# Ranking edges by source bucket in half chunks: the match tile in PSUM, a predicated copy for product and addition

## The reference, cut to what matters

```python
src, dst = (edge_index[0], edge_index[1])
msg_input = jnp.concatenate([x[src], x[dst], edge_attr], axis=-1)
h = jax.nn.relu(msg_input @ W1.T + b1)
messages = h @ W2.T + b2
agg = jax.ops.segment_sum(messages, dst, num_segments=x.shape[0])
upd = jax.nn.relu(agg @ Wu.T + bu)
y = x + upd
```

## Time and profile before

| | us |
|---|---|
| median of 3 runs (lowest, highest) | 6159.68 (6158.24, 6160.03) |
| span of the profiled execution | 6159.3 |
| starts of the first and the last gather of the edge MLP | 1456.1, 2644.6 |
| starts of the first and the last match of the ranking | 1466.1, 2500.5 |

### The profile page before, as it was taken

How to read it: one execution, slowest core, us unless ns; L and a number is a source line. 1 busy time by engine, 2 the same in 40 slices (tenths; PEclk the granted TensorE clock), 3 DMA queues, 4 the chain that set the end, 5 groups by cost and what they waited for, 6 DMA issues and landing times. The chain is left out here.

```text
span 6159.3 us, 93437 instructions
## 1 busy us (share of the span) xinstructions
PE 3901.9 (63%) x20652; PEld 3181.0 (52%) x20652; DVE 3661.3 (59%) x11663; ACT 2833.9 (46%) x6936; POOL 4388.1 (71%) x4477
## 2 busy tenths in 40 slices
PE   5567766765666666768878877334444346766665
PEld 4566666654555555545655555233333346665443
DVE  6788888886888888767777675111101124445665
ACT  3788888881111111255555554111111148784443
POOL 3676777654777777757777776677777777777775
PEclk8787887787888888878898887555555569898877
DMA  4444444454645555542222224322222235553223
GB/s 125 124 132 126 129 128 127 127 103 125 171 133 136 139 136 134 145 66 73 74 74 74 74 74 66 96 77 76 76 75 75 74 108 167 163 165 88 58 58 46
DMA packets 485366, 649.31 MB, mean 105 GB/s; under 512 B 120187, under 2 KB 332938, under 8 KB 484822
## 3 DMA queue, kind: packets, MB, share of 16 engines
q0 software_dynamic: 155552, 345.75, 22.1%
q1 hardware_dynamic: 329271, 297.58, 17.7%
HBM read 495.44 MB, written 150.71 MB: 105 GB/s over the span
## 5 line engine op out<-in xcount | busy, mean ns | idle before, releaser
L692 POOL DMA_INDIRECT e_ring<-table,gather_i x880 | 921.5, 1047 | 287.3 <-issue 267.5
L692 POOL DMA_INDIRECT kv_ring<-keys_values,gather_i x880 | 864.1, 982 | 365.2 <-issue 248.0
L2099 POOL DMA_INDIRECT rows_by_src<-arena,key x880 | 870.9, 990 | 310.2 <-issue 260.3
L692 POOL DMA_INDIRECT e_ring<-filter_rows,gather_i x880 | 840.7, 955 | 304.5 <-issue 268.1
L692 POOL DMA_INDIRECT arena<-table,gather_i x880 | 858.7, 976 | 278.9 <-issue 265.9
L2083 PE MATMUL rs_ph<-nodes,arena 128*128 x1664 | 424.4, 436 | 668.1 <-ACT arena L2092 615.2
L2083 PEld LDWEIGHTS rs_ph<-nodes,arena 128*128 128x128 f32 x1664 | 365.7, 324 | 727.4 <-issue 727.2
L2075 DVE TENSOR_SCALAR arena<-arena,part 128x512 f32<-128x512 bf16 x220 | 113.2, 518 | 949.0 <-PE rs_ph L2083 898.8
L1562 PE MATMUL e_pa<-e_msg,e_hot 128*128 128x128 f32 x3520 | 559.9, 311 | 35.8 <-DVE e_msg L1764 28.2
L741 DVE TENSOR_TENSOR arena<-arena,e_pa 128x128 f32 x1760 | 495.0, 281 | 114.0 <-PE e_pa L1562 68.9
L2325 PE MATMUL gl_sum_f<-arena,gl_hot_f 128*128 128x128 f32 x1760 | 283.0, 311 | 425.0 <-DMA arena<-table,gather_i 191.0
(11 more groups left out here) (461 smaller groups left out, 9863.7 us busy)
## 6 DMA issues: line engine op xcount, KB each, us to landing
rows_by_src<-e_filler SPq DMA_DIRECT2D x256, 260.0 KB
arena<-rows_by_src SPq DMA_DIRECT2D x256, 260.0 KB
at_rows<-local_rows SPq DMA_DIRECT2D x220, 128.0 KB, 3.5
e_rows<-local_rows SPq DMA_DIRECT2D x220, 128.0 KB
arena<-local_rows SPq DMA_DIRECT2D x220, 128.0 KB, 3.3
e_attr<-edge_attr SPq DMA_DIRECT2D x880, 25.0 KB
kv_ring<-keys_values,gather_i POOLq DMA_INDIRECT x880
e_ring<-table,gather_i POOLq DMA_INDIRECT x880
```

The lines of the kernel that those rows point to most:

```text
L692: pool.indirect_dma_start(ring[:, r, u, :], None, table, bass.IndirectOffsetOnAxis(index, 0)).then_inc(arrived[r], 16)
L2099: pool.indirect_dma_start(self.table, bass.IndirectOffsetOnAxis(place, 0), self.out[:, r, u, :], None, bounds_check=SLOTS_R - 1, oob_is_er ...
```

## The change

The row of 832 columns is ranked in two halves of 416 (`HCHUNK`). For each half there are three instructions: the match, now written to a PSUM tile; the scan, which reads the match there and starts the second half from the last rank of the first; and a predicated copy, which writes the rank into `slot_of` where the match isn't zero (no two buckets mark the same edge, so a copy does what product and addition did). That is six instructions a bucket in the same four steps: in an even step the match comes ahead of all the step's other work and the scan at its end, in an odd step the copy comes at its end. Each still waits for the one before.

The match tile takes a bank of PSUM. `pn` goes from four banks to three: the result of `project` moves into columns 128 to 255 of the bank of `turn_nodes`. `turn_nodes` waits in addition until `keep_rows` of the bucket before has read it. SP's wait at batch 204 is for a count of 297 instead of 199.

```diff
--- before.py
+++ after.py
@@ -18,6 +18,7 @@
 F32 = mybir.dt.float32
 I32 = mybir.dt.int32
 BF16 = mybir.dt.bfloat16
+U32 = mybir.dt.uint32
 ALU = mybir.AluOpType
 ACT = mybir.ActivationFunctionType
 AX_X = mybir.AxisListType.X
@@ -82,6 +83,7 @@
 VALS0 = ACC_N
 LINKS0 = VALS0 + VALS * U * F
 RANKS0 = B1_0
+HCHUNK = CHUNK // 2
 SPOTS0 = RANKS0 + 5 * CHUNK
 NUMBERS0 = SPOTS0 + JC * P
 assert RANKS0 + 4 * TILES <= SPOTS0 and NUMBERS0 + 3 * TILES <= QUERY0
@@ -1321,7 +1323,7 @@
 
             filler, filled = sb("filler", [P, U, REV]), sem("filled")
             src_i = arena(c, RANKS0, [CHUNK], I32)
-            src_bucket, slot_of, match, rank = (arena(c, RANKS0 + n * CHUNK, [CHUNK]) for n in range(1, 5))
+            src_bucket, slot_of, rank = (arena(c, RANKS0 + n * CHUNK, [CHUNK]) for n in range(1, 4))
             sources, ranked, slotted, spotted = sem("sources"), sem("ranked"), sem("slotted"), sem("spotted")
             phase, whole = (arena(c, NUMBERS0 + n * TILES, [TILES]) for n in range(2))
             cut, sined = sem("cut"), sem("sined")
@@ -1329,7 +1331,8 @@
             sums, sums_t, plus, mid, y, t, z, x_new, x_t = (sb(n, [P, P]) for n in ("sums", "sums_t", "plus", "mid", "y", "t", "z", "x_new", "x_t"))
             keep = sb("keep", [P, 3, F])
             stat, mean, root = sb("stat", [P, 2, 6]), sb("mean", [P, 2, 2]), sb("root", [P, 2, 2])
-            pn = pb("pn", [P, 4, 512])
+            pn = pb("pn", [P, 3, 512])
+            match = pb("match", [P, 512])[:, 0:HCHUNK]
             joined, summed_t, copied_t, updated, added_x, moments, rooted = (sem(n) for n in ("joined", "summed_t", "copied_t", "updated", "added_x", "moments", "rooted"))
             shifted, moments2, renewed, turned_x, copied_x, projected, kept, held = (
                 sem(n) for n in ("shifted", "moments2", "renewed", "turned_x", "copied_x", "projected", "kept", "held"))
@@ -1398,7 +1401,7 @@
                     sp.dma_start(to, attr_dram[:, bass.ds(e0[u], P)]).then_inc(attributes[r], 16)
                 if layer == 1:
                     if k == R * NB + 8:
-                        sp.wait_ge(ranked, 3 + 4 * NB)
+                        sp.wait_ge(ranked, 3 + 6 * NB)
                         sp.dma_start(c.slots.rearrange("(p n) -> p n", p=P), slot_of).then_inc(slotted, 16)
                     if is_first(k):
                         sp.wait_ge(start, 3)
@@ -1480,7 +1483,7 @@
                 act.wait_ge(projected, n + 1)
                 at_least(act, row_sent[n % 3], 16 * (n // 3), None)
                 at_least(act, held, n - 2, None)
-                act.activation(keep[:, n % 3, :], pn[:, 3, 0:F], ACT.Copy).then_inc(kept, 1)
+                act.activation(keep[:, n % 3, :], pn[:, 2, P:P + F], ACT.Copy).then_inc(kept, 1)
 
             def soften_nodes(k, i, r):
                 n = BUCKET_AT.get(k)
@@ -1588,6 +1591,7 @@
                     return
                 pe.wait_ge(renewed, 2 * n + 1)
                 at_least(pe, copied_x, n, None)
+                at_least(pe, kept, n, None)
                 pe.transpose(pn[:, 2, 0:P], x_new[:, :], c.ident[:, :]).then_inc(turned_x, 1)
 
             def project(k, i, r):
@@ -1596,7 +1600,7 @@
                     return
                 pe.wait_ge(copied_x, n + 1)
                 at_least(pe, kept, n, None)
-                pe.matmul(pn[:, 3, 0:F], x_t[:, :], c.w["lin1"][:, :], start=True, stop=True).then_inc(projected, 1)
+                pe.matmul(pn[:, 2, P:P + F], x_t[:, :], c.w["lin1"][:, :], start=True, stop=True).then_inc(projected, 1)
 
             def mix(k, i, r):
                 n = BUCKET_AT.get(k)
@@ -1659,16 +1663,16 @@
                 dve.wait_ge(ranked, 2)
                 dve.tensor_scalar(slot_of, src_bucket, float(NB), float(4 * SLOTS), ALU.is_ge, ALU.mult).then_inc(ranked, 1)
 
-            def rank_bucket(b, part):
-                dve.wait_ge(ranked, 3 + b * 4 + part)
+            def rank_bucket(b, half, part):
+                dve.wait_ge(ranked, 3 + b * 6 + half * 3 + part)
+                of = slice(half * HCHUNK, half * HCHUNK + HCHUNK)
+                before_it = c.base[:, b:b + 1] if half == 0 else rank[:, HCHUNK - 1:HCHUNK]
                 if part == 0:
-                    ins = dve.tensor_scalar(match, src_bucket, c.j[:, b:b + 1], None, ALU.is_equal)
+                    ins = dve.tensor_scalar(match, src_bucket[:, of], c.j[:, b:b + 1], None, ALU.is_equal)
                 if part == 1:
-                    ins = dve.tensor_tensor_scan(rank, c.ones[:, 0:1].broadcast_to([P, CHUNK]), match, c.base[:, b:b + 1], ALU.mult, ALU.add)
+                    ins = dve.tensor_tensor_scan(rank[:, of], c.ones[:, 0:1].broadcast_to([P, HCHUNK]), match, before_it, ALU.mult, ALU.add)
                 if part == 2:
-                    ins = dve.tensor_tensor(rank, rank, match, ALU.mult)
-                if part == 3:
-                    ins = dve.tensor_tensor(slot_of, slot_of, rank, ALU.add)
+                    ins = dve.copy_predicated(slot_of[:, of], match.bitcast(U32), rank[:, of])
                 ins.then_inc(ranked, 1)
 
             def number(n):
@@ -1838,6 +1842,8 @@
                 new = not (isinstance(k, int) and k >= BATCHES)
                 there = lambda n: (not isinstance(k, int) or n <= k < BATCHES + n)
                 steps = []
+                if layer == 1 and k < R * NB and r % 2 == 0:
+                    rank_bucket(k // R, r // 2, 0)
                 if layer == 1 and new:
                     steps.append(lambda: one_hot_turned(k, i, r))
                 if layer == 2 and there(2):
@@ -1851,7 +1857,7 @@
                     return Adds(nc, dve, acc, buckets, pa[:, ra % 2, :, :], F, ka, summed, added, tick)
                 between(adds if there(add_lag) else None, steps)
                 if layer == 1 and k < R * NB:
-                    rank_bucket(k // R, r)
+                    rank_bucket(k // R, r // 2, 1 + r % 2)
                 if layer == 1 and CUT_AT <= k < CUT_AT + 4:
                     cut_off(k - CUT_AT)
                 if layer == 1 and CUT_AT + 8 <= k < CUT_AT + 10:
```

## The result

| | us |
|---|---|
| before, median of 4 runs beside it | 6159.85 |
| changed, median of 4 runs (lowest, highest) | 6080.08 (6069.62, 6084.35) |
| ratio, with its 95% interval | 0.9867 (0.9856 to 0.9879) |
| span of the profiled execution, the quickest of the four | 6067.6 |
| starts of the first and the last gather of the edge stage | 1451.6, 2564.3 |

A forecast was written before the change was run, and what follows sets the result against it. POOL's 880 gathers, one after another, were taken to bound the second layer's edge stage, stretched by DVE's ranking. 79 us less there and nothing elsewhere: 6159.7 - 79 = 6081 us, range 6067 to 6122 us.

The forecast's parts named there:

- The step that carried the forecast: Second layer's edge stage: 771 gathers in the ranking window fall from 1058 to 955 ns, 79.4 us off POOL.
- 2566 us: Sign that the forecast is right: the edge stage's last gather starts near this time, against 2644.6 us before.
- the same clock: Edge stage, 2520 to 2600 us: gathers after ranking take 955 ns with clock unchanged and no less DMA traffic.
- the rival in which PSUM frees nothing: Ranking pieces still stall gathers, but shorter ones less: 26 us gained, 6133 us; chance 0.06.
- the bounds: Ranking on DVE, per half: match 0.34 to 1.04 us, predicated copy 0.59 to 1.04 us.
- DVE's reserve: Ranking window: DVE's time to spare against POOL's pace shrinks from 0.7 to 0.34 us a batch.
- wanted it halved: Sign that the forecast is right: DVE's idle before its edge-stage sum (L1759), 132.1 us before, halves.
- the rival in which DVE becomes the pace: Copy and match cost their upper ends, DVE needs 5.15 us a batch: 58 us gained, 6102 us; chance 0.16.
- The copy doesn't hold the port: Rival: the predicated copy still holds the port, reading what it overwrites: 11 us of stall, 6092 us; chance 0.15.
- The slow copy: Rival: a predicated copy of 2.5 us makes DVE 39 us slower, 6198 us; chance of slower 0.05.
- The bank cost nothing: Node results sharing a PSUM bank: 2 us of room, at most 13 us of PE time, costed at nothing.

The follow-up runs named there:

- e7: Kernel before with only the predicated copy, over all 832 columns, replacing product and addition, match in SBUF: 6153.41 us, ratio 0.9994.
- e3: Changed kernel with product and addition, in halves, instead of the predicated copy, match still in PSUM: 6080.68 us, ratio 0.9874.
- e5: Changed kernel plus two unused additions of 416 columns a bucket, one input in PSUM, the other in SBUF: 6084.47 us, ratio 0.9869.
- e4: Changed kernel plus one unused addition of 832 columns a bucket, inputs and output in SBUF: 6103.28 us, ratio 0.9894.
- e1: Changed kernel with only the match tile moved back to SBUF, halves and predicated copy kept: 6109.36 us, ratio 0.9920.
- e9: Changed kernel with the last stage's row of column numbers copied once into PSUM for its one-hot comparison: 6057.42 us, ratio 0.9829.
- e10: The changed kernel itself, run again on the same chip as e9 as its measure: 6079.4 us, ratio 0.9865.
- e6: Changed kernel plus three unused additions in each half, one operand in PSUM: 6142.55 us, ratio 0.9962.
- e8: Match, product and addition in SBUF as in the kernel before, but in halves of 416 and the change's order: 6130.23 us, ratio 0.9935.
- e2: Kernel before with only the shared PSUM bank and its added wait, ranking untouched: 6162.76 us, ratio 1.0003.

## Why the prediction was right

**The bound and the stall.** The step that carried the forecast was 771 x (1058 - 955) ns = 79.4 us on POOL. The stage shortened by 76 us, the gathers by 1058 - 960 = 98 ns each, and the median of the runs by 79.8 us. The last start came at 2564.3 us, where 2566 us was named. That the forecast of the whole time is met to 1 us is luck: 76 us are the stage's, the other 4 us lie elsewhere, and the runs of the changed kernel spread over 15 us. e7 shows that DVE work taken away brings nothing, e3 and e5 that DVE work added costs nothing, and e4 that a pass with all operands in SBUF does. With only the memory changed, e1 loses 34 us in the stage and e9 gains 26 us in the last one. The rule of the Trainium skill (SBUF — State Buffer, section "SBUF: two separate sides") agrees with all of these, e1 against the changed kernel and e9 against e10 above all; that section names no predicated copy, and e7 adds one with mask and data in SBUF, 0.55 us of stall a copy.

The prediction read "the same clock" behind the ranking; its own rows have 0.87 there and 0.83 within. The clock isn't what shortens a gather: it takes 954 ns in e6 at a granted clock of 0.86 and 1062 ns in e7 at 0.85.

**What the prediction didn't separate.** It put the whole gain down to the port being freed. The runs split it. Cutting into halves alone gives 0.9935, a third to a half (e8); putting the match in PSUM as well gives the rest (e3, 0.9874); the copy gives nothing on top (the changed kernel's 0.9867 lies within e3's interval). The prediction did see that "shorter ones stall less", in the rival in which PSUM frees nothing, but priced it at 26 us of gain; e1 shows a gain of 49 us (0.0080 x 6160; 42 us in the stage of its profiled execution), since a scan of 1.07 us cost 0.28 us and a match or copy under 0.09 us.

**The prices on DVE.** Match 0.59 us taken, 0.64 us measured; copy 0.59 and 0.62 us; scan 1.04 and 1.07 us: all within the bounds; the prices were 3 to 8% low. The match in SBUF takes 0.43 us in e1 for the same columns, so PSUM costs it 0.21 us, which agrees with the Trainium skill (VectorE: DVE Perf Modes, section "Why PSUM operands drop a tier"); I had reckoned 0.25 us.

**DVE's reserve.** Forecast 4.70 us of need against a pace of 5.04 us, 0.34 us in reserve. Measured: a batch takes 4 x (0.960 + 0.305) = 5.06 us, and 0.43 us of it is idle before the sum. That is 37% less than before, where the prediction wanted it halved. e3 used nearly all of it and lost nothing, and e6 went past it and lost 65 us in the stage. So the rival in which DVE becomes the pace was a real one, but takes over 0.43 us a batch more than the change asks.

**The other rivals.** The copy doesn't hold the port when its mask is in PSUM: over the timeline the gathers beside the copies are 0.5 us above their median in all, where 11 us were priced. The slow copy fell with its 0.62 us. The bank cost nothing (e2), and in the trace of the changed kernel nothing but DVE's node result is waited for before the transpose.

## What to carry to other kernels

Where indirect DMAs issued by GpSimd set the pace, look at the spread of their durations, not at GpSimd's busy share: a minimum far under the mean, with slow ones that began under a DVE pass, may be time that DVE takes from them. Here it was so for passes with both inputs in SBUF, and in small part for the match with its input and output there. A free bank of PSUM for one operand of such a pass took the stall away; writing the match there cost DVE time (0.64 us for 0.43 us), reading it there did not. And DVE time is free until its idle time before the dependent sum is used up. Cutting the passes in two, with their order changed, gave a third to a half of the gain here with no PSUM at all.

## What the runs showed of the hardware that was not expected

- A gather is exposed to a pass with both inputs in SBUF at its start only, and then it waits for the pass to end. In the trace of before, a gather that begins under a product or an addition ends 0.82 us after that pass does, and one that begins under a scan 0.75 us after it, however much of the pass was left, from 0.25 us up (middle 80% of 65 and of 53 gathers: within 0.01 us). Where the pass begins more than 0.15 us after the gather, the gather is 0.02 us above the median on average (140 gathers). In e1 and e8 the scans give 0.75 us again.
- So a stall grows faster than the pass that causes it: a shorter pass is less often under way when a gather begins, and less of it is then left. Per scan it is 0.97 us at 1.94 us (before), and 0.28 us (e1) to 0.38 us (e8) at 1.07 us. The difference between the last two shows that the phase between passes and gathers counts too.
- The change leaves 15 us of gather time above the median, 11 us of it on gathers beside no ranking instruction, where before had 4 us on those. No run tried what brings them.
- The granted clock of PE from 1600 to 2400 us is 0.85 or 0.86 in before, e2, e7 and e6, whose batches take about 5.4 us, and 0.89 to 0.91 in the changed kernel (0.91, and 0.89 in e10), e3 and e5, whose batches take 5.05 us. PE isn't busy for more of the time there: 553 of 800 us in before and in the changed kernel alike. No run tried what raises it.
- Runs of the changed kernel spread over 15 and 19 us (changed and e10), those of e9 over 6 us. Four runs each don't settle it, but the last stage's length (1117.6 and 1125.3 us in two profiled executions of one kernel) points to the meetings of its comparison with the gathers as one source.
